# Two flamingo layers on one core: maxima of two score banks merged, w1's rounding constant on ScalarE, all orders rewritten

## The chip, the cores and the metric

One core of one Trainium2 chip. The metric is the device time of one execution of the kernel in microseconds, the median of several runs. Weights are raw inputs: their quantization and splitting are part of the time.

## The reference, cut to what matters

x is [2, 2048, 512] in float32. Two layers follow each other, each with a cross attention or mixing block and a feed-forward block, added with gates:

```python
x = x + tanh(g_xattn[0]) * attention(layernorm(x), ctx, Wq, Wkv, Wout)   # 8 heads, rotary, 128 context rows
x = x + tanh(g_ffn[0]) * ffn_relu2(layernorm(x), w_fc, w_proj, u, v, fast_b, gate)   # ternary weights, low rank part
x = x + tanh(g_xattn[1]) * (layernorm(x) @ W1.T + mean(ctx) @ W2.T + b)
x = x + tanh(g_ffn[1]) * bitlinear(gelu(bitlinear(layernorm(x), w1, b1)), w2, b2)
```

The score step is softmax(q k^T / 8) over the 128 context rows. In the last block bitlinear rounds its input, after an rms norm, to integers of -127 to 127 by the row's largest absolute value, and the weights to -1, 0 and 1.

## The kernel before, in words

The 4096 rows are worked in 16 groups of 256 rows, each of two tiles of 128 rows. For every group the steps are: layer norm 1, q projection, rotation, scores, softmax, values (pv), output projection (wo), layer norm 2, the low-rank part (low, low_sum), the up projection with relu squared in 8 chunks (up and up_rest), the down projection in 4 pieces per tile, layer norm 3, the mix projection (wx), layer norm 4 and rounding (x3_out, q4_out), w1 in 4 steps per tile, gelu and rounding, w2, and the store. Where float32 precision is wanted a tensor is kept as a high and a low part in float16, and three products are added. All the products write into 8 banks of PSUM.

Five engines work from five lists written out by hand: TensorE, VectorE (DVE), ScalarE (ACT), GpSimd (POOL), and the queue of SyncE (SP), which issues all loads, stores and DMA transposes. The table ORDER (from L334) gives for each engine, each step and each group the places of its tiles in that engine's list, and PREP the places of the preparation steps; each run() walks through the places and calls the step. Steps of three or four neighbouring groups are interleaved in this way, with the preparation of the weights (rounding to ternary, "lift" and "clip", the copy of lowA, the high part of wx) interleaved with groups 0 and 1. Every dependency is a semaphore wait in the step itself (need() and need_dma()), so that an engine that arrives early stands still, with its whole list behind it.

The steps that the change touches are these.

- Scores and softmax. `scores` (L1760) writes 4 units of scores into 4 banks, the four of each matmul round next to each other. `soft_max` (L1408, L1412) takes on VectorE for each unit the negated maximum of 4 heads and multiplies it by the scale; `exps` (L966) waits for the unit and takes 4 exponentials on ScalarE, and sums them. Then follow reciprocal, product on GpSimd (L781), float16 copy (L974), low part (L1382), and a DMA transpose ahead of pv.
- Ahead of the scores stands the rotation: three products on VectorE (L1395 to L1398), a sum on GpSimd (L771), the high part on ScalarE (L959), and the low part on VectorE (L1382).
- Rounding ahead of w1. `x3_out` (L1476 and on) adds the mix to the rows and takes statistics; `q4_out` scales the row (L1489 to L1496), multiplies it and adds 12582912 so that it is rounded (L1505), and subtracts the constant again into float16 (L1509). SP then transposes the result (`turn_q4`), and `w1_up` (L1904) uses it. `x3_hi` (L1023) is ScalarE's float16 copy of a tile of the same size. In the last group the transposes are done by TensorE (L1647), and the constant is subtracted by ScalarE behind them (L908).
- `ln3_apply` (L1378) writes the tile x3n that the rounding of the group before has read.

The other lines that come up: L1735 q projection, L1788 output projection, L1434 its sum on VectorE, L1801 and L1810 the low-rank matmuls with ScalarE's copies (L988, L992) and VectorE's rest (L1447), L1835 and L1841 up, L1002 relu on ScalarE, L1861 down, L776 low part of the hidden tile on GpSimd, L1883 mix, L1920 w2, L1556 the last sum of a tile.

Of the kernel before, what the change touches and what calls it, by code (L numbers as in the profile page):

```python
# [19 lines left out]
ACT = mybir.ActivationFunctionType  # L20
# [3 lines left out]
P = 128  # L24
# [24 lines left out]
def build(nc, x_d, ctxT_d, wqT_d, wkvT_d, woT_d, wfc_d, wproj_d, uT_d, wxT_d, wcT_d, bx_d, w1T_d, b1_d, w2T_d, b2_d,  # L49
          rope_d, small_d, out_d):  # L50
    ctx = ExitStack()
    with ctx:
# [173 lines left out]
        def mix_bank(g, n):  # L226
# [47 lines left out]
        turned_x3, turned_q4, turned_q5, end_x3lo, end_q4 = [sem(n) for n in (  # L274
            "turned_x3 turned_q4 turned_q5 end_x3lo end_q4").split()]
# [55 lines left out]
        def last_in(place):  # L331
# [18 lines left out]
                down=((45, 46, 48, 49, 47, 50, 51, 53), (77, 78, 81, 85, 80, 87, 89, 93),  # L350
# [13 lines left out]
                wo=((26, 27), (54, 55), (90, 91), (125, 126), (166, 167), (204, 205), (242, 243), (282, 283),
                    (320, 321), (361, 362), (399, 400), (438, 439), (476, 478), (517, 518), (558, 559), (594, 595)),
                low=((33,), (61,), (95,), (133,), (174,), (211,), (251,), (289,), (330,), (369,), (408,), (447,),
                     (486,), (524,), (564,), (603,)),
                wx=((58, 59), (94, 110), (136, 147), (172, 184), (216, 225), (250, 267), (292, 306), (333, 338),
                    (372, 379), (410, 418), (448, 457), (484, 497), (523, 537), (567, 575), (601, 606), (635, 636)),
                w1=((73, 74, 75, 76, 79, 82, 83, 86), (111, 112, 113, 115, 119, 120, 124, 130),  # L370
# [225 lines left out]
        def _(sp):  # L596
# [1408 lines left out]
```

## Time and profile before

| what | us |
|---|---|
| median of 3 runs | 1177.62 |
| lowest, highest | 1175.28, 1179.0 |
| the profiled execution, its own time | 1178.83 |
| its span in the profile | 1176.7 |
| TensorE busy in it | 1094.3 |
| VectorE busy | 953.5 |
| ScalarE busy | 799.4 |
| GpSimd busy | 591.5 |

The profile is of one execution. Busy times are shares of its span, 1176.7 us; the rest of the execution's own time, 2.1 us, lies around the span. A group of rows names a line of the kernel, the engine, what is written and read, the count, the busy time, the mean duration and the idle time just before, with the engine that ended it.

### The profile page before, as it was taken

The page shows a single profiled execution, that of the slowest core. Times are in us where ns is not written, and L with a number is a line of the kernel's source. Part 1 is how long each engine was busy: PE and PEld are TensorE (multiplying, and loading weights), DVE is VectorE, ACT ScalarE, POOL GpSimd, SP SyncE. Part 2 cuts the span into 40 slices and gives each one's busy share as a digit, 9 for nine tenths or more (in the row PEclk, how much of TensorE's full clock was granted, in tenths as well). Part 3 has the DMA queues.
Part 4 walks back from the last instruction along what each step waited for, and adds up shares of the span by engine and source line. Part 5 has one row for each costly group of instructions (what it writes and reads, how often), then busy time and mean ns, then how long its engine had stood idle before and what let it go on. Part 6 is the DMA issues. An engine that isn't in the chain of part 4 may idle for free.

```text
span 1176.7 us, 22172 instructions
## 1 busy us (share of the span) xinstructions
PE 1094.3 (93%) x8270; PEld 677.4 (58%) x8558; DVE 953.5 (81%) x1989; ACT 799.4 (68%) x1575; POOL 591.5 (50%) x567
## 2 busy tenths in 40 slices
PE   5776699999999999999899999999999999999997
PEld 5544456474655656475655656475656656564654
DVE  4796868778789888788878798898879886998667
ACT  3988947676683958576584857676674957586545
POOL 4243545464653746454544656555545555564431
PEclk9888799999999999999999999999999999999999
DMA  9959651434525343533625252443436242432210
GB/s 339 367 153 309 204 122 47 99 81 77 126 59 117 69 116 73 104 81 68 126 53 136 57 123 68 89 110 77 108 55 145 45 119 61 103 69 55 68 45 27
DMA packets 273802, 128.11 MB, mean 109 GB/s; under 512 B 247568, under 2 KB 248080, under 8 KB 272016
## 3 DMA queue, kind: packets, MB, share of 16 engines
q1 hardware_dynamic: 273136, 125.73, 41.8%
q8 instruction: 67, 1.10, 0.4%
q10 hardware_dynamic: 560, 0.96, 0.3%
q14 instruction: 39, 0.32, 0.1%
HBM read 57.19 MB, written 8.39 MB: 56 GB/s over the span
## 4 chain that ended last, share of the span: by engine, by line
PE 55%; ACT 17%; DVE 16%; POOL 5%; issue 4%; DMA 2%; SPq 0%; ACTq 0%; DVEq 0%
PE ps L1861 14%; PE ps L1835 10%; PE ps L1904 6%; PE ps L1920 5%; PE ps L1788 5%; ACT e L966 4%; PE ps L1735 4%; PE ps L1883 4%; ACT rl L1002 3%; ACT hid L1007 2%; ACT sq L1013 2%; PE ps L1760 1%; DVE st L1369 1%; PE ps L1841 1%; PE ps L1775 1%
## 5 line engine op out<-in xcount | busy, mean ns | idle before, releaser
L1835 PE MATMUL ps<-xT,fcT 128*128 128x256 f16 x2048 | 262.5, 276 | 10.8 <-ACT rl L1002 7.1
L749 POOL TENSOR_TENSOR rs<-ve,nhalf 128x1 f32<-128x1 f32 x160 | 101.7, 638 | 306.1 <-DVE ve L1374 222.8
L1861 PE MATMUL ps<-pjT,hid 128*128 128x512 fp8e4 x1024 | 232.3, 379 | 2.6 <-POOL hid L776 1.6
L1835 PEld LDWEIGHTS ps<-xT,fcT 128*128 128x128 fp8e4 x2048 | 200.1, 99 | 52.6 <-ACT rl L1002 10.0
L776 POOL TENSOR_TENSOR hid<-sq,hid 128x512 f16<-128x512 f32 x128 | 163.1, 1279 | 80.3 <-ACT sq L1013 79.4
L1861 PEld LDWEIGHTS ps<-pjT,hid 128*128 128x128 f16 x1024 | 98.0, 98 | 98.3
L1002 ACT ACTIVATE rl<-ps,rsf 128x256 f32<-128x256 f32 x256 | 106.4, 469 | 25.0 <-PE ps L1841 24.8
L966 ACT ACTIVATE e<-ps,nmb,sig 128x128 f32<-128x128 f32 x256 | 113.1, 462 | 7.2 <-DVE nmb L1412 6.9
L1904 PE MATMUL ps<-w1T,q4T 128*128 128x512 fp8e4 x480 | 114.2, 379 | 0.7 <-issue 0.6
L1058 ACT ACTIVATE q<-h 128x2048 f16<-128x2048 f32 x30 | 57.3, 1910 | 79.3 <-DVE h L1531 79.3
L781 POOL TENSOR_TENSOR e<-e,einv 128x512 f32<-128x512 f32 x64 | 70.1, 1100 | 78.5 <-DVE einv L1416 78.5
L1520 DVE SCALAR_TENSOR_TENSOR h<-ps,dqs,b1bc 128x512 f32<-128x512 f32 x120 | 87.4, 744 | 27.0 <-PE ps L1904 24.4
L1920 PE MATMUL ps<-w2T,hT 128*128 128x512 fp8e4 x480 | 108.5, 379 | 0.7 <-DMA hT<-q 0.7
L1735 PE MATMUL ps<-pt,wq 128*128 128x256 f16 x768 | 88.6, 275 | 4.4 <-DVE r L1434 3.0
L1788 PE MATMUL ps<-wo,qT 128*128 128x512 f16 x384 | 87.3, 384 | 4.4 <-DVE qT L1382 4.4
L1735 PEld LDWEIGHTS ps<-pt,wq 128*128 128x128 f16 x768 | 75.3, 99 | 18.4 <-issue 7.8
L1883 PE MATMUL ps<-wx,xT 128*128 128x512 f16 x360 | 82.5, 379 | 2.3 <-DVE r L1556 1.2
L1007 ACT ACTIVATE hid<-rl 128x512 f16<-128x512 f32 x128 | 80.6, 630 | 5.0
L1100 DVE TENSOR_REDUCE amax<-h 128x1 f32<-128x2048 f32 x30 | 68.4, 2280 | 13.4 <-ACT h L1027 13.3
L1013 ACT ACTIVATE sq<-rl 128x512 f32<-128x512 f32 x128 | 78.5, 613 | 0.0
L1920 PEld LDWEIGHTS ps<-w2T,hT 128*128 128x128 f16 x480 | 46.2, 98 | 50.7
L1382 DVE TENSOR_TENSOR p<-e,p 128x512 f16<-128x512 f32 x64 | 62.6, 993 | 14.0 <-ACT p L974 13.7
(243 smaller groups left out, 2025.7 us busy)
## 6 DMA issues: line engine op xcount, KB each, us to landing
xb<-in_x SPq DMA_DIRECT2D x16, 512.0 KB, 3.6
xa<-in_x SPq DMA_DIRECT2D x15, 512.0 KB, 4.0
out<-r SPq DMA_DIRECT2D x30, 256.0 KB, 2.3
rope<-in_rope SPq DMA_DIRECT2D x16, 384.0 KB, 3.2
h<-in_w1T SPq DMA_DIRECT2D x6, 1024.0 KB, 5.8
h<-in_w2T SPq DMA_DIRECT2D x6, 1024.0 KB, 6.4
h<-in_wkvT SPq DMA_DIRECT2D x2, 1024.0 KB, 12.6
hid<-in_w_fc SPq DMA_DIRECT2D x2, 1024.0 KB, 9.9
```

The costliest lines, as they stand in the source:

```text
L776: pool.tensor_tensor(flat[:, 1, :], sq[:, m % 2, :], flat[:, 0, :], ALU.subtract).then_inc(hid_lo, 1)
L966: last = act.activation(e[:, n, a * S:(a + 1) * S], s_bank(g, n)[:, a * S:(a + 1) * S], ACT.Exp, bias=nmb[:, n, a:a + 1], scale=sig[:, :], ...
L1002: act.activation(rl[:, m % 2, a * G:(a + 1) * G], ps[:, FFN0 + m % 2, a * G:(a + 1) * G], ACT.Relu, scale=rsf[:, 2 * m + a:2 * m + a + 1]) ...
L1007: act.activation(hid[:, 0, 2 * m:2 * m + 2, :].rearrange("p c n -> p (c n)"), rl[:, m % 2, :], ACT.Square)\
L1013: act.activation(sq[:, m % 2, :], rl[:, m % 2, :], ACT.Square).then_inc(sq_done, 1)
L1735: mm = pe.matmul(q_bank(hg)[:, a * G:(a + 1) * G], wq[:, ws, k, c:c + P], xT1[:, xs, k, :], start=(n == 0 and k == 0), stop=(n == 2 and k ...
L1788: mm = pe.matmul(wo_bank(t), ao[:, xs, k, t * P:(t + 1) * P], wo[:, ws, k, :], start=(n == 0 and k == 0), stop=(n == 2 and k == KC - 1))
L1835: pe.matmul(ps[:, FFN0 + m % 2, a * G:(a + 1) * G], fcT[:, k, f * P:(f + 1) * P], xT2[:, xs, k, :], start=(xs == 0 and k == 0), stop=False)
L1861: mm = pe.matmul(ps[:, FFN0 + t, :], hid[:, xs, c, t * P:(t + 1) * P], pjT[:, c, :], start=(c == 0 and xs == 0), stop=(c == FC - 1 and xs ...
L1883: mm = pe.matmul(mix_bank(g, t), xT3_of(g)[:, xs, k, t * P:(t + 1) * P], wx[:, ws, k, :], start=(n == 0 and k == 0), stop=(n == 2 and k == ...
L1904: mm = pe.matmul(mix_bank(g, 2 + u), q4T_of(g)[:, k, t * P:(t + 1) * P], w1T[:, k, n * 512:(n + 1) * 512], start=(k == 0), stop=(k == KC - 1))
L1920: mm = pe.matmul(mix_bank(g, 10 + t), hT_of(g)[:, t, c, :], w2T[:, c, :], start=(c == 0), stop=(c == FC - 1))
```

## The change

Three things are changed. The maxima of the third and fourth bank of scores (banks 2 and 3 of PSUM, which lie next to each other) are taken by one reduction of 128x1024 and one product, which raises the semaphore by two. The subtraction of the rounding constant ahead of w1 is taken from VectorE and done by ScalarE, as a copy with a bias, for all groups under one semaphore, q4_int; SP waits for it ahead of the transpose, and so does ln3_apply of the next group ahead of writing x3n. Every place in ORDER and PREP is written anew.

```diff
@@ -176,6 +176,9 @@
         return back_bank(g - 2, 0)
     return ps[:, ROW_TILES[j], :]
 
+def s_pair():
+    return slice(ROW_TILES[2], ROW_TILES[3] + 1)
+
 def pv_bank(a):
     return ps[:, (4, 2)[a], :]
 
@@ -271,8 +274,8 @@
 xT1_in, xT2_in, xT3_in, q4T_in, hT_in = [[sem(f"{n}{t}") for t in range(TILES)] for n in
                                          "xT1_in xT2_in xT3_in q4T_in hT_in".split()]
 p_in = [sem(f"p_in{n}") for n in range(4)]
-turned_x3, turned_q4, turned_q5, end_x3lo, end_q4 = [sem(n) for n in (
-    "turned_x3 turned_q4 turned_q5 end_x3lo end_q4").split()]
+turned_x3, turned_q4, turned_q5, end_x3lo, q4_int = [sem(n) for n in (
+    "turned_x3 turned_q4 turned_q5 end_x3lo q4_int").split()]
 END = GROUPS - 1
 TURN_Q5 = (0, 1, 5, 6)
 
@@ ORDER, TensorE @@
-s=((13,), (31,), (60,), (106,), (146,), (182,), (221,), (261,), (299,), (335,), (374,), (412,),
-   (451,), (494,), (536,), (571,)),
+s=((13,), (31,), (66,), (103,), (146,), (181,), (218,), (261,), (300,), (337,), (377,), (414,),
+   (456,), (493,), (537,), (571,)),
...
@@ ORDER, ScalarE @@
+q4=((90, 91), (128, 134), (158, 172), (196, 205), (229, 238), (264, 274), (296, 311), (332, 341),
+    (360, 368), (396, 406), (430, 443), (471, 475), (501, 513), (538, 546), (565, 573), (577, 579)),
...
@@ -662,7 +666,7 @@
         if final(g):
             return
         need(sp, w1_ps, 4 * TILES, g - 1, 4 * t + 3)
-        need(sp, q4_done, 2 * TILES, g, 2 * t + 1)
+        need(sp, q4_int, TILES, g, t)
         sp.dma_start_transpose(q4T[:, :, t * P:(t + 1) * P], q4[:, t, :]).then_inc(q4T_in[t], 16)
 
     def turn_q5(g, t):
@@ -903,10 +907,6 @@
                            accum_out=scf[:, done:done + 1]).then_inc(c_rows, 1)
 
     def prepare(p):
-        for t in here("ACT", "q4_end", p):
-            act.wait_ge(turned_q4, t + 1)
-            act.activation(q4T_of(END)[:, :, t * P:(t + 1) * P], chunks_of(FFN0 + t), ACT.Copy, bias=-MAGIC)\
-                .then_inc(end_q4, 1)
         for _ in here("ACT", "wq", p):
             weight_hi(0, 0, wq32, wq)
         for _ in here("ACT", "k_hi", p):
@@ -1022,6 +1022,15 @@
         need(act, xn3, TILES, g, t)
         act.activation(x16b[:, t, 0, :], x3n_of(g)[:, t, :], ACT.Copy).then_inc(x3hi, 1)
 
+    def q4_integers(g, t):
+        if final(g):
+            act.wait_ge(turned_q4, t + 1)
+            dst, src = q4T_of(g)[:, :, t * P:(t + 1) * P], chunks_of(FFN0 + t)
+        else:
+            need(act, q4_done, TILES, g, t)
+            dst, src = q4[:, t, :], x3n[:, t, :]
+        act.activation(dst, src, ACT.Copy, bias=-MAGIC).then_inc(q4_int, 1)
+
     def gelus(g, t):
         need(act, h_done, 4 * TILES, g, 4 * t + 3)
         act.activation(h_of(g)[:, t, :], h_of(g)[:, t, :], ACT.Gelu).then_inc(gelu, 1)
@@ -1079,6 +1088,8 @@
                 low_first(g)
             for t, g in due("ACT", "x3_hi", p):
                 x3_hi(g, t)
+            for t, g in due("ACT", "q4", p):
+                q4_integers(g, t)
             for t, g in due("ACT", "gelu", p):
                 if final(g):
                     gelu_quarters(g, t)
@@ -1403,13 +1414,18 @@
         lo(flat[:, 1, :], ropeu[:, hg, :], flat[:, 0, :], q_lo)
 
     def soft_max(g, n):
-        need(dve, s_ps, 4, g, n)
-        scores = s_bank(g, n).rearrange("p (h s) -> p h s", h=4)
-        dve.tensor_reduce(nmx[:, n, :], scores, axis=AX.X, op=ALU.max, negate=True).then_inc(s_max, 1)
+        units = slice(2, 4) if n == 2 else slice(n, n + 1)
+        need(dve, s_ps, 4, g, units.stop - 1)
+        if n == 2:
+            scores = ps[:, s_pair(), :].rearrange("p b (h s) -> p b h s", h=4)
+        else:
+            scores = s_bank(g, n).rearrange("p (h s) -> p h s", h=4).unsqueeze(1)
+        dve.tensor_reduce(nmx[:, units, :], scores, axis=AX.X, op=ALU.max, negate=True).then_inc(s_max, 1)
         if first(g) and n == 0:
             dve.wait_ge(c_kap, 1)
-        need(dve, s_max, 4, g, n)
-        dve.tensor_scalar(nmb[:, n, :], nmx[:, n, :], sig[:, :], None, ALU.mult).then_inc(s_bias, 1)
+        need(dve, s_max, 3, g, n)
+        dve.tensor_scalar(nmb[:, units, :], nmx[:, units, :], sig[:, :], None, ALU.mult)\
+            .then_inc(s_bias, units.stop - units.start)
 
     def soft_inv(g, n):
         need(dve, s_exp, 4, g, n)
@@ -1463,6 +1479,7 @@
         ln_stats(ln3, g, 2, t, r2_of(g)[:, t, :], 1.0, EPS)
 
     def ln3_apply(g, t):
+        need(dve, q4_int, TILES, g - 1, t)
         ln_apply(rs3, xn3, g, 2, t, r2_of(g)[:, t, :], x3n_of(g)[:, t, :])
 
 
@@ -1503,10 +1520,6 @@
         quant_scales(z4, 6 * t + 2, 6 * TILES, 0, g, t, rs4, 3, wmean[:, 0:1])
         z = x3n_of(g)[:, t, :]
         dve.tensor_scalar(z, z, qsc[:, 0, t:t + 1], MAGIC, ALU.mult, ALU.add).then_inc(q4_done, 1)
-        if final(g):
-            return
-        need(dve, q4_done, 2 * TILES, g, 2 * t)
-        dve.tensor_scalar(q4[:, t, :], z, MAGIC, None, ALU.subtract).then_inc(q4_done, 1)
 
     def h_out(g, t, n):
         need(dve, w1_ps, 4 * TILES, g, 4 * t + n)
@@ -1654,14 +1667,14 @@
             turn(FFN0 + t, x3n_of(END)[:, t, :], turned_x3)
         for t in here("PE", "q4_turn", p):
             pe.wait_ge(end_x3lo, t + 1)
-            need(pe, q4_done, 2 * TILES, END, t)
+            need(pe, q4_done, TILES, END, t)
             turn(FFN0 + t, x3n_of(END)[:, t, :], turned_q4)
         for u in here("PE", "q5_turn", p):
             t, n = u // 4, u % 4
             if t == 1:
                 need(pe, q5_done, TILES, END, n)
             elif n < 2:
-                pe.wait_ge(end_q4, n + 1)
+                need(pe, q4_int, TILES, END, n)
             else:
                 need(pe, out_done, TILES, END - 1, 1)
             need(pe, q5_round, TILES, END, u)
@@ -1896,7 +1909,7 @@
         elif not final(g) and not final(g + 1):
             need(pe, s_exp, 4, g + 2, 1)
         if n == 0 and final(g):
-            pe.wait_ge(end_q4, t + 1)
+            need(pe, q4_int, TILES, g, t)
         elif n == 0:
             need_dma(pe, q4T_in[t], g)
         pe.ldweights(q4T_of(g)[:, 0, t * P:(t + 1) * P], tile_position=(0, 0))
```

The tables, read as a sequence, give for TensorE between some steps (group behind the point; the steps stand in the order of the list):

```
between q1.8 and s.8:          before up1.7 up_rest1.7 up2.7             after up1.7 up_rest1.7 up2.7 up3.7
between low_sum and up1:       before nothing in 0, 13                   after nothing in 2, 12, 14
between wo1.2 and low.2:       before w2_0.0 down7.1 wx0.1               after down5.1 down6.1 w2_0.0 down7.1 wx0.1 q0.3 q1.3
between wx1.8 and w1_4.8:      before w1_0.8 w1_1.8 up3.9 up4.9 up5.9 up6.9 up7.9 w1_2.8 pv0.10 down0.9 w1_3.8
                               after  up2.9 up3.9 w1_0.8 w1_1.8 w1_2.8 w1_3.8 up4.9
from the last down step, before: x3_turn0 w2_0.14 x3_turn1 wx0.15 wx1.15 w2_1.14 q4_turn0 w1_0.15 w1_1.15 w1_2.15 q4_turn1
                               w1_3.15 w1_4.15 w1_5.15 w1_6.15 w1_7.15 q5_turn0..3 w2_0.15 q5_turn4..7 w2_1.15
from the last down step, after: wx0.15 w1_4.14 w1_5.14 w1_6.14 w1_7.14 x3_turn1 w2_0.14 wx1.15 q4_turn0 w1_0.15 w1_1.15 w1_2.15
                               w1_3.15 q4_turn1 w1_4.15 w1_5.15 w1_6.15 w1_7.15 w2_1.14 q5_turn0..3 w2_0.15 q5_turn4..7 w2_1.15
```

## Rows read from the trace of the kernel before

**Rows 1.** The page, busy time, share of the span and instructions of each engine

```profile
PE 1094.3 (93%) x8270; PEld 677.4 (58%) x8558; DVE 953.5 (81%) x1989; ACT 799.4 (68%) x1575; POOL 591.5 (50%) x567
```

**Rows 2.** Windows of three stages; columns: stretch, length, busy of PE, PEld, DVE, ACT, POOL, PEclk, DMA

```profile
0.00:150.00 150.00, 104.19 (x759) 73.63 (x761) 107.73 (x209) 119.00 (x228) 61.98 (x60) 0.86 0.83 273
150.00:1120.00 970.00, 941.92 (x7274) 577.82 (x7539) 807.04 (x1691) 654.65 (x1303) 517.52 (x494) 1.00 0.38 88
1120.00:1176.70 56.70, 48.14 (x242) 25.98 (x259) 38.74 (x91) 25.70 (x46) 12.03 (x14) 0.97 0.13 38
```

**Rows 3.** What TensorE waited for, 150 to 1120 us; columns: total, times, longest

```profile
PE ps L1760 <- DVE qT L1382: 5.9, 7, 2.0
PE ps L1835 <- ACT rl L1002: 2.9, 5, 1.4
PE ps L1788 <- DVE qT L1382: 2.6, 3, 1.1
...
PE ps L1861 <- POOL hid L776: 1.6, 3, 1.2
PE ps L1735 <- DVE r L1434: 1.5, 2, 0.9
...
PE ps L1883 <- DVE r L1556: 1.2, 2, 0.9
...
PE ps L1835 <- DVE tres L1447: 0.9, 1, 0.9
...
PE ps L1904 <- issue: 0.6, 1, 0.6
```

**Rows 4.** Groups by form; busy, mean ns, then idle before

```profile
L1408 DVE TENSOR_REDUCE nmx<-ps 128x4 f32<-128x512 f32 x64 | 43.6, 681 | 11.8 <-PE ps L1760 11.8
...
L1412 DVE TENSOR_SCALAR nmb<-nmx,sig 128x4 f32<-128x4 f32 x64 | 25.7, 401 | 2.4
...
L1509 DVE TENSOR_SCALAR x16b<-x3n 128x512 f16<-128x512 f32 x30 | 24.5, 817 | 1.0
...
L1023 ACT ACTIVATE x16b<-x3n 128x512 f16<-128x512 f32 x30 | 18.8, 626 | 53.6 <-DVE x3n L1378 53.6
...
L1100 DVE TENSOR_REDUCE kvmax<-ps 128x1 f32<-128x1024 f32 x1 | 1.2, 1225 | 0.5 <-PE ps L1684 0.5
```

**Rows 5.** Line 1509 alone: ns at least, median, at most

```profile
L1509 DVE TENSOR_SCALAR x16b<-x3n x30: 426/428/1376, 187.7 to 1103.8; 128x512 f16<-128x512 f32 x30
```

**Rows 6.** Timeline of group 8 ahead of its scores; columns: start, length, instructions

```profile
580.69 1.46 POOL L771 TENSOR_TENSOR e<-e 128x512 f32<-128x512 f32 x1
581.05 1.38 DVE L1509 TENSOR_SCALAR x16b<-x3n 128x512 f16<-128x512 f32 x1
...
583.78 2.48 PE L1760 MATMUL ps<-k,qT 32*128 32x128 f16 x96 [2.03 <-DVE qT L1382]
```

**Rows 7.** The chain of waits, one unit's exps on ScalarE

```profile
458.91 1.76 ACT e L966 x8
```

**Rows 8.** The chain by time, 210 to 240 us; columns: start, length, what

```profile
218.38 1.73 PE ps L1861 x8
...
235.90 2.05 issue
```

**Rows 9.** TensorE's timeline in group 13, behind the low-rank sum

```profile
963.27 1.05 PE L1835 MATMUL ps<-xT,fcT 128*128 128x256 f16 x8 [0.94 <-DVE tres L1447]
```

**Rows 10.** What TensorE waited for, 0 to 150 us

```profile
PE ps L1835 <- ACT rl L1002: 4.2, 2, 2.7
```

**Rows 11.** The window from 120 to 150 us, columns as rows 2

```profile
120.00:150.00 30.00, 22.28 (x153) 16.46 (x155) 23.82 (x23) 29.76 (x61) 17.59 (x11) 0.77 0.75 208
```

**Rows 12.** Timeline of TensorE in the tail

```profile
1144.43 3.62 PE L1920 MATMUL ps<-w2T,hT 128*128 128x512 fp8e4 x16
...
1151.82 0.60 PE L1647 MATMUL ps<-ident,e 128*128 128x128 f32 x4
...
1161.31 3.44 PE L1647 MATMUL ps<-ident,hid 128*128 128x128 f32 x16 [4.47 <-DVE hid L1550]
```

More of the change, by code:

```diff
@@ L364, in build @@
[L364 to L369, printed above, removed]
@@ new lines, in build @@
+                low_sum=((33,), (61,), (99,), (135,), (175,), (215,), (252,), (291,), (332,), (371,), (411,),
+                         (450,), (489,), (525,), (567,), (603,)),
+                up_rest=((36, 37), (64, 65), (101, 102), (138, 139), (178, 180), (219, 220), (256, 258), (293, 297),
+                         (335, 336), (375, 376), (413, 416), (452, 454), (491, 492), (528, 529), (569, 570),
+                         (606, 607)),
+                up=((34, 35, 38, 39, 40, 42, 43, 44), (62, 63, 67, 68, 76, 78, 79, 80),
[7 rows of a table added]
@@ new lines, in build @@
+                wo=((24, 26), (54, 55), (88, 89), (127, 128), (165, 166), (204, 205), (242, 243), (281, 282),
+                    (320, 321), (361, 362), (400, 401), (439, 440), (478, 479), (516, 517), (558, 560), (595, 596)),
+                low=((32,), (60,), (97,), (133,), (173,), (214,), (250,), (289,), (330,), (369,), (409,), (448,),
+                     (487,), (523,), (565,), (601,)),
+                wx=((56, 59), (94, 107), (136, 148), (176, 185), (216, 224), (257, 266), (292, 306), (331, 341),
+                    (367, 378), (406, 418), (444, 458), (484, 497), (526, 539), (564, 576), (604, 615), (629, 636)),
@@ L545, in build @@
                        (329, 330))))
         PREP = dict(
-            PE=dict(x3_turn=(632, 634), q4_turn=(638, 642), q5_turn=(648, 649, 650, 651, 653, 654, 655, 656),
-                    k=(2, 3), v=(5, 6), low=(0,), mix=(14,), tern=(4, 10, 11, 15, 19, 20, 21, 22), low_t=(16,),
-                    row_scale=(24,), mean=(30,), spread=(1, 8, 12, 18, 25)),
-            DVE=dict(x3lo_end=(814, 817), ctx_sum=(7,), rot_k=(10, 11), wq_max=(3,), wq_scale=(6,), k_max=(13,),
-                     wq_lo=(8,), v_max=(19,), kv_scale=(23,), k_lo=(29,), v_lo=(34, 35), low_copy=(5,),
-                     thr=(9, 15, 20, 37, 46, 48, 49, 52), wo_max=(12,), v_top=(22,), wo_scale=(26,), wo_lo=(30,),
-                     mix_row=(43,), low_rank=(42,), v_parts=(28,), wx_max=(53,), hidden=(54,), wx_scale=(58,),
-                     wx_lo=(88,), row_scale=(56,), mean=(71,), diag=(55,), round=(72, 78, 81, 89, 90, 95, 97, 101),
-                     clip=(79, 85, 86, 91, 94, 98, 100, 103)),
@@ L556, in build @@
-            ACT=dict(q4_end=(548, 549), wq=(3,), k_hi=(17,), v_hi=(19, 20), tanh=(1,), wo=(18,),
-                     evac=(6, 14, 15, 29, 33, 35, 36, 37), rows=(4, 7, 10, 21), whole=(5, 8, 12, 28), low=(32,),
-                     wx=(46,), sums=(39, 40, 41, 42, 43, 44, 45, 47), lift=(54, 61, 62, 67, 71, 76, 79, 80)),
-            POOL=dict(whole=(18, 19, 20, 21), rot_k=(5, 6), csb=(4,), low_zero=(13,)),
-            SP=dict(u=(0,), rows=(16,), ctx=(2,), wk=(3,), wq=(1,), wv=(7,),
-                    piece=(4, 5, 10, 18, 19, 15, 22, 24, 27, 29, 31, 32, 33, 36, 37, 38, 40, 41, 45, 47, 48, 50, 52, 55),
-                    wo=(6,), wc=(14,), wx=(13,), b1=(17,)))
+            PE=dict(x3_turn=(627, 634), q4_turn=(637, 642), q5_turn=(648, 649, 650, 651, 653, 654, 655, 656),
+                    k=(2, 3), v=(5, 6), low=(0,), mix=(14,), tern=(4, 9, 10, 15, 17, 18, 19, 21), low_t=(22,),
+                    row_scale=(30,), mean=(29,), spread=(1, 11, 12, 23, 25)),
@@ new lines, in build @@
+            DVE=dict(x3lo_end=(790, 799), ctx_sum=(13,), rot_k=(9, 10), wq_max=(3,), wq_scale=(6,), k_max=(12,),
+                     wq_lo=(7,), v_max=(18,), kv_scale=(24,), k_lo=(28,), v_lo=(26, 36), low_copy=(5,),
+                     thr=(8, 14, 20, 35, 43, 44, 47, 48), wo_max=(11,), v_top=(23,), wo_scale=(25,), wo_lo=(31,),
+                     mix_row=(49,), low_rank=(51,), v_parts=(30,), wx_max=(53,), hidden=(54,), wx_scale=(69,),
+                     wx_lo=(80,), row_scale=(75,), mean=(64,), diag=(55,), round=(67, 72, 78, 86, 90, 91, 94, 102),
+                     clip=(73, 83, 87, 88, 92, 97, 99, 104)),
@@ new lines, in build @@
+            ACT=dict(wq=(3,), k_hi=(18,), v_hi=(17, 19), tanh=(1,), wo=(20,), evac=(6, 13, 14, 31, 32, 33, 35, 36),
+                     rows=(4, 7, 9, 21), whole=(5, 8, 11, 28), low=(48,), wx=(53,),
+                     sums=(38, 39, 40, 41, 42, 43, 45, 46), lift=(52, 61, 66, 67, 72, 78, 79, 82)),
+            POOL=dict(whole=(18, 19, 20, 21), rot_k=(4, 5), csb=(6,), low_zero=(13,)),
+            SP=dict(u=(0,), rows=(13,), ctx=(2,), wk=(3,), wq=(1,), wv=(5,),
+                    piece=(4, 7, 11, 20, 19, 16, 22, 24, 28, 30, 31, 32, 35, 36, 37, 38, 39, 42, 45, 47, 49, 50, 52, 55),
+                    wo=(6,), wc=(18,), wx=(14,), b1=(17,)))
```

258 lines of the change are left out of this document (127 added, 131 removed), and 123 rows, old and new, of tables (down, exp, h, hid).

## The prediction

> **What bounds the kernel now.** I read the busy shares first, then a table by stage, then what TensorE waited for. TensorE is busy 93% of the span, VectorE 81%, ScalarE 68% [rows 1]. The stages say more [rows 2]: the first 150 us, in which weights are loaded and quantized, leave TensorE idle for 150.0 - 104.2 = 45.8 us; the 970 us from 150 to 1120 leave it idle for only 28.1 us; the last 56.7 us for 8.6 us. The granted clock is 1.00 in the long middle, which is the 2.4 GHz level, and 0.86 in the first stage. All orders are rewritten but TensorE does the same matmuls, so a new order can win only from idle time and from the clock of the first stage. In the middle the pot is 28 us, spread over many waits of 0.2 to 2 us [rows 3]: 5.9 for the low part of q ahead of the scores, 2.6 for the low part ahead of the output projection, 2.9 for ScalarE's relu, 0.9 in the low-rank chain, and so on down to single DMA or issue waits. So this is a TensorE-bound kernel with thin stalls, and a VectorE that is cheaper by some per cent saves nothing by itself.
>
> **Part 1, rounding constant to ScalarE.** VectorE loses 30 subtractions at 817 ns, 24.5 us; ScalarE gains 30 copies with a bias. The nearest row is the copy of the same tile and shape at 626 ns, 18.8 us [rows 4]. Over the middle ScalarE works 654.7 of 970 us, so 18.8 us more fit; VectorE falls from 807 towards 783 us. What is late on the path is another matter. The chain is x3_out, statistics, q4_out, integers, transpose, w1. It now has one more hand-over, but 0.63 us in place of 0.82. The mean of 817 ns hides two cases: the median is 428 ns, the longest 1376 ns [rows 5]. In group 8's timeline the instruction starts at 581.05 inside a GpSimd addition (580.69 to 582.15), takes 1.38 us and ends 0.28 us after it; the low part of q stands behind it on VectorE, and TensorE then sits 2.03 us ahead of the scores [rows 6]. 30 x (817 - 428) = 11.7 us of VectorE's 24.5 are such waits. The page SBUF — State Buffer of the Trainium skill, section "SBUF: two separate sides", says that VectorE and GpSimd share one port pair under an exclusive lock, so that either blocks the other for a whole instruction. By that rule GpSimd gets time back too, and the gain would be the third rival's and not mine; the trace agrees as far as VectorE's side goes, 1.38 against 0.43 us.
>
> New waits: the transpose of q4 on SP waits for ScalarE instead of VectorE, and behind it in SP's queue stand the next transposes. ln3_apply of the next group now waits for ScalarE's integers of this one, with all of VectorE's list behind it; those integers precede this group's w1, whose results VectorE needs long before that, so I cost it at 0. Without that cover it is 0.63 us per tile. The last group's integers were on ScalarE before: 0.
>
> **Part 2, one maximum for banks 3 and 4.** 16 times, two reductions of 681 ns and two products of 401 ns become one of each. The reduction of 128x1024 from PSUM stands in the trace once, at 1225 ns [rows 4], so it saves 16 x (2 x 681 - 1225) = 2.2 us; the products save 16 x 401 = 6.4 us. The four banks of scores are finished by neighbouring matmuls, so no wait is added. The third exp starts 1225 - 681 = 0.54 us later and the fourth earlier; the unit before keeps ScalarE busy for 1.76 us [rows 7] and covers that. If ScalarE sat idle there it would cost 16 x 0.54 = 8.7 us at worst; VectorE's saving lies beside TensorE: 0 on the path. Both parts take 24.5 + 8.6 = 33.1 us (3.5%) from VectorE.
>
> **Part 3, the orders.** This decides. No row shows the new order, so I measured each dependency by its cover: the TensorE steps listed between producer and user, at the chain's rates (8 down matmuls of 512 columns 1.73 us [rows 8], so 0.216 each and 0.108 for 256 columns; an up chunk has 18 of these, 1.95). Against cover stands the latency seen in the old order.
> - q to scores: cover on the mean of groups 1 to 14 from 5.2 to 6.5 us, the smallest from 1.5 to 3.0. Group 8, 2.03 us late, gets one more up chunk (1.95). I take -3.0 of the 5.9; ends -5.9 and 0.
> - Values to output projection: smallest cover 0.9 to 1.7, mean 3.0 to 3.3: -1.3 of 2.6; ends -2.6 and +1.
> - Low-rank chain: the second up chunk stands right behind low_sum in one group before (13, a wait of 0.94 us [rows 9]) and in three now (2, 12, 14): +2.0; ends 0 and +3.
> - Output projection to low: smallest cover 7.7 before (group 2, 2.05 us of issue in the chain [rows 8]), 8.5 now (3 and 15): 0; ends -2 and +3.
> - Other places where VectorE is the releaser (1.5 + 1.2 + 0.9 [rows 3]), with 3.5% less before it: -1.5; ends -3.6 and 0.
> - Start: TensorE waits 4.2 us there for the relus of group 0 [rows 10], ScalarE being busy 29.76 of the 30 us from 120 [rows 11]. The new list of ScalarE has one 2.0 us lift and one p_hi fewer ahead of the last relu, but moves the copy of lowA and wx's high part towards that place: -2.0; ends -6 and +4.
> - Tail: the second w2 of group 14 now stands between the last w1 and the turns of q5, where TensorE waits 4.47 us [rows 12], and lasts 3.45: up to -3.5. But four w1 steps of group 14 come after the last down steps of group 15, and between the last mix and the second q4 turn there are now one turn and four w1 steps, 0.45 + 4 x 0.86 = 3.9 us; in the old order this stretch ran from 1144.43 to 1151.82, 7.4 us, with a w2 in it. I take +1.0; ends -3.5 and +5.
> Sum: -3.0 - 1.3 + 2.0 - 1.5 - 2.0 + 1.0 = -4.8, say -5. It is made against the profiled execution, 1178.83 us (span 1176.7), which stands 1.2 us above the median of the runs: 1177.6 - 5 = 1172.6 us.
>
> **Rivals.** About 0.3% (3.5 us) is what a measurement of this kernel can tell from no change: 1174.1 to 1181.2 is "same".
> - *New stalls in place of old ones*: the old order's 28 us in the middle are single waits at changing places; a rewritten order has its own. For it: VectorE is the releaser of 5.9 + 2.6 + 1.5 + 1.2 + 0.9 = 12.1 us of the 28.1; three zero covers stand where one was. Against: the covers of the two largest VectorE waits grew. Time: 1177.6.
> - *Slower: the w1 matmuls wait for ScalarE.* The integers now stand in ScalarE's list behind a unit's exps (1.76 us [rows 7]) or a gelu. In the old order covers down to 10.5 us between wx and w1 of tile 1 left no wait but 0.6 us of issue [rows 3]; in the new one the smallest are 9.2 (group 8), 10.2 (2), 10.5 (1 and 5), 11.1 (3 and 11). If each integer step comes 2.0 us late, they lack 3.3 + 2.3 + 2 x 2.0 + 2 x 1.4 = 12.4 us: 1172.6 + 12.4 = 1185. From 1.4 us of lateness (8.8 us) it outweighs my gain by enough to be read as slower. Against: ScalarE is idle 315 of the middle's 970 us [rows 2], and the copy is 0.19 us shorter than the subtraction that it replaces [rows 4].
> - *Larger gain*: if VectorE's instructions have slowed GpSimd's as GpSimd's slow VectorE's, both become faster, and all waits of the middle on q, wo, r, tres and hid vanish: 5.9 + 2.6 + 1.5 + 1.2 + 0.9 + 1.6 = 13.7; with start and tail as above, 14.7: 1163. For it: an instruction of 428 ns that takes up to 1376. Against: hid's waits have been 1.6 us only. The lock in the page named above would work this way.
> - That the change doesn't do what it says: the exps read the merged result by unit as before, so I see no room for it, and give it nothing.
>
> **Numbers.** Forecast (1167 to 1174) 0.40, larger gain 0.12, same 0.32, slower 0.16. So faster 0.52. The range 1163 to 1183 leaves out half of the large gain and most of the slower case, about 0.15. The likeliest case's own range is 1167 to 1174.
>
> **What would show it.** VectorE busy near 920 us and ScalarE near 818; the fp16 subtraction gone, a 626 ns copy in its place; 16 reductions near 1.2 us. Idle of TensorE in the middle near 24 us, waits ahead of the scores near 3 us. The tail: no 4.5 us wait at the turns of q5, a new one of some 3 us at q4's. I am wrong if w1 waits for q4T, if the zero covers cost over 1 us each, or if the first stage moves by more than 5 us.

## The result, and the profile after

The changed kernel takes 1183.37 us (median of 6 runs, 1182.73 to 1184.83) beside 1176.24 for the one before in the same session: ratio 1.0062, 95% interval 1.0045 to 1.0079. It is slower by some 7 us. The prediction was 1172.6, faster. The profiled execution took 1184.36 us, with a span of 1182.2.

The page of the changed kernel, its busy shares:

```profile
span 1182.2 us, 22186 instructions
PE 1092.8 (92%) x8270; PEld 670.5 (57%) x8558; DVE 927.5 (78%) x1927; ACT 814.7 (69%) x1605; POOL 577.7 (49%) x567
```

The parts did most of what was foreseen. VectorE lost 26.0 us against [rows 1], not the 33.1 forecast; ScalarE gained 15.3; TensorE did the same work. The next view groups the instructions by form (line, output <- input, count, busy time, mean ns, idle before), first ScalarE, then VectorE:

```profile
L1032 ACT ACTIVATE x16b<-x3n 128x512 f16<-128x512 f32 x30 | 18.7, 624 | 9.0 <-DVE x3n L1522 9.0
...
L1423 DVE TENSOR_REDUCE nmx<-ps 128x4 f32<-128x512 f32 x32 | 21.9, 684 | 14.3 <-PE ps L1773 14.2
L1423 DVE TENSOR_REDUCE nmx<-ps 128x8 f32<-128x1024 f32 x16 | 19.4, 1213 | 0.0
L1427 DVE TENSOR_SCALAR nmb<-nmx,sig 128x4 f32<-128x4 f32 x32 | 17.3, 542 | 1.2
L1427 DVE TENSOR_SCALAR nmb<-nmx,sig 128x8 f32<-128x8 f32 x16 | 5.5, 345 | 1.7
```

The integers take ScalarE 624 ns a tile where 626 was taken for them, and the merged maximum 1213 where 1225 was taken. The small products saved 2.9 us and not 6.4 (17.3 + 5.5 against 25.7 [rows 4]): one for a single bank takes 542 ns on the mean here, 401 before. The stages, in the columns of [rows 2]:

```profile
0.00:150.00 150.00, 101.25 (x756) 72.41 (x756) 103.52 (x200) 113.92 (x216) 53.60 (x58) 0.89 0.82 261
150.00:1120.00 970.00, 939.70 (x7259) 572.32 (x7522) 776.54 (x1619) 670.96 (x1341) 512.29 (x496) 1.00 0.38 89
1120.00:1182.20 62.20, 51.79 (x258) 25.80 (x281) 47.47 (x109) 29.81 (x49) 11.84 (x14) 1.00 0.13 36
```

TensorE is idle for 48.8 us in the first stage (45.8 before), 30.3 in the middle (28.1; forecast 24) and 10.4 behind it (8.6). The first stage was hardly slower for it (by 0.6 us, in the table below): its granted clock is 0.89 in place of 0.86. What TensorE waited for between 150 and 1120 us (us in total, times, longest), against [rows 3]:

```profile
PE ps L1773 <- DVE qT L1393: 5.1, 3, 4.0
PE ps L1814 <- issue: 3.8, 5, 1.2
PE ps L1848 <- DVE tres L1463: 3.1, 4, 1.0
PE ps L1896 <- DMA xT<-x16b: 2.3, 2, 1.3
PE ps L1874 <- issue: 2.3, 1, 2.3
PE ps L1848 <- ACT rl L1002: 2.3, 3, 1.4
PE ps L1896 <- DVE r L1569: 2.1, 4, 0.9
PE ps L1917 <- DVE h L1533: 2.0, 3, 1.1
PE ps L1748 <- DVE r L1450: 1.8, 1, 1.8
...
PE ps L1801 <- DVE qT L1393: 1.1, 2, 0.6
```

The many short waits ahead of the scores (7) became 3, but one of them is 4.0 us long. Of the four waits in the low-rank chain, three stand at the zero covers of groups 2, 12 and 14 (0.93, 0.94 and 1.03 us in TensorE's timeline), the fourth is 0.22. No row above blames ScalarE for more than it did before, and the whole view has no wait for q4T: from it alone nobody would find the cause.

To see where the time goes I use **lost time**: at a mark, the time minus what the matmuls done until then would take at the chain's full rate (0.216 us for 512 columns; float32 ones weighted fourfold). All kernels here do the same matmuls, so only differences between kernels are read from it. Worked out from the matmul groups up to each mark:

| mark, us | 150 | 200 | 650 | 1100 | end of span |
|---|---|---|---|---|---|
| before | 38.4 | 42.5 | 76.7 | 98.5 | 105.3 |
| changed kernel | 39.0 | 49.4 | 73.8 | 102.3 | 110.8 |

The changed kernel loses 6.3 us between 150 and 200, gains 9.8 until 650, and loses 6.7 between 650 and 1100.

### The profile page after: what moved, and what is told of

It reads as the page before. It is cut to its first block, busy times and chain, and to the rows that moved or that the text cites. A ratio compares the mean times of both kernels' runs of the same rounds, so it can differ in the third digit from the quotient of the medians.

```text
span 1182.2 us, 22186 instructions
## 1 busy us (share of the span) xinstructions
PE 1092.8 (92%) x8270; PEld 670.5 (57%) x8558; DVE 927.5 (78%) x1927; ACT 814.7 (69%) x1605; POOL 577.7 (49%) x567
## 4 chain that ended last, share of the span: by engine, by line
PE 56%; DVE 17%; ACT 16%; issue 5%; DMA 4%; POOL 1%; SPq 0%; ACTq 0%; POOLq 0%; DVEq 0%
PE ps L1874 14%; PE ps L1848 11%; PE ps L1917 6%; PE ps L1801 5%; PE ps L1933 5%; PE ps L1748 4%; ACT e L966 4%; PE ps L1896 4%; ACT rl L1002 2%; ACT hid L1007 2%; DVE st L1380 2%; ACT sq L1013 1%; PE ps L1854 1%; PE ps L1788 1%; DMA h<-in_w2T 1%
## 5 line engine op out<-in xcount | busy, mean ns | idle before, releaser
L1848 PE MATMUL ps<-xT,fcT 128*128 128x256 f16 x2048 | 261.0, 275 | 7.9 <-ACT rl L1002 4.5
L1848 PEld LDWEIGHTS ps<-xT,fcT 128*128 128x128 fp8e4 x2048 | 197.6, 98 | 51.9 <-ACT rl L1002 8.3
L780 POOL TENSOR_TENSOR hid<-sq,hid 128x512 f16<-128x512 f32 x128 | 155.4, 1217 | 102.3 <-ACT sq L1013 101.9
L1393 DVE TENSOR_TENSOR p<-e,p 128x512 f16<-128x512 f32 x64 | 64.8, 1022 | 26.0 <-ACT p L974 25.7
```

What stands on the lines that cost most here:

```text
L780: pool.tensor_tensor(flat[:, 1, :], sq[:, m % 2, :], flat[:, 0, :], ALU.subtract).then_inc(hid_lo, 1)
L1848: pe.matmul(ps[:, FFN0 + m % 2, a * G:(a + 1) * G], fcT[:, k, f * P:(f + 1) * P], xT2[:, xs, k, :], start=(xs == 0 and k == 0), stop=False)
```

## The experiments

Each is timed beside the kernel before, whose median was 1176.0 to 1177.9 in the five sessions, so the ratios are what is compared. A run's label stands where it is introduced. "Old orders" are those of the kernel before, "new orders" those of the changed one; "the constant" is w1's rounding constant.

**Orders and parts taken apart.** First the new orders with neither part (e_orders): VectorE subtracts, four maxima.

```diff
-q4_integers(g, t) on ScalarE for every group
+dve.tensor_scalar(q4[:, t, :], z, MAGIC, None, ALU.subtract).then_inc(q4_int, 1)   # behind q4_out's rounding
-one reduction of s_pair()
+soft_max(g, 2); soft_max(g, 3)
```

> The new orders of every engine, with neither of the other two parts: the maxima are taken bank by bank again (the third and fourth at the same place), and VectorE takes the rounding constant off again. Theory 'the orders lose it': with VectorE 33 us busier the new orders do no better than in the changed kernel, 1184 to 1189 us. Theory 'ScalarE's extra step in the chain loses it': without it the new orders are at or under the time of before, 1172 to 1178 us.

Measured: 1189.97 us, ratio 1.0108 [1.0091, 1.0126]. Then the reverse (e_parts), both parts in the old orders, each of ScalarE's copies put into its list where the subtraction had ended in the trace of before:

```diff
 ORDER = the old places
-dve.tensor_scalar(q4[:, t, :], z, MAGIC, None, ALU.subtract)
+act.activation(q4[:, t, :], x3n[:, t, :], ACT.Copy, bias=-MAGIC).then_inc(q4_int, 1)
+the merged soft_max(g, 2)
```

> The old orders with both parts: one maximum for the third and fourth bank at the place of the third, and ScalarE taking the constant off at the place in its old list that came next once VectorE's rounding had ended in the trace of before. Theory 'the orders lose it': the parts alone are harmless or help, 1170 to 1176 us. Theory 'ScalarE's extra step loses it': 1180 to 1186 us, with waits ahead of w1 or of the scores.

Measured: 1186.38, ratio 1.0086 [1.0069, 1.0102]. So the parts cost in the old orders, and the new orders cost without the parts; together they cost far less than the sum of the two.

**The two parts one by one**, in the old orders. The merged maximum alone (e_max):

```diff
 ORDER = the old places
-soft_max(g, 2); soft_max(g, 3)
+the merged soft_max(g, 2)
```

> The old orders with the merged maximum alone. The old orders with both parts took 1186.4 us, 9.5 over before. Theory 'ScalarE's list': this part adds nothing to ScalarE, so 1173 to 1179 us. Rival 'the later third exp': the third exp starts 0.5 us later in 16 groups, so 1180 to 1186 us.

Measured: 1176.28, ratio 0.9987 [0.9973, 1.0000]. Nothing that can be told from none, as costed. The constant on ScalarE alone (e_int):

```diff
 ORDER = the old places
-dve.tensor_scalar(q4[:, t, :], z, MAGIC, None, ALU.subtract)
+act.activation(q4[:, t, :], x3n[:, t, :], ACT.Copy, bias=-MAGIC).then_inc(q4_int, 1)
```

> The old orders with the rounding constant taken off by ScalarE alone. Theory 'ScalarE's list': the copy of 0.63 us, and the wait for VectorE ahead of it, stand in front of relus that TensorE needs at the pace of one chunk in 1.95 us while ScalarE takes 2.18 us for one, so this part carries nearly all of the 9.5 us: 1183 to 1187 us. Rival 'both parts share it': 1180 to 1182 us. Rival 'the merged maximum': 1175 to 1179 us.

Measured: 1185.64, ratio 1.0067 [1.0049, 1.0084]. This is the part that costs. TensorE's waits in the middle of this run (its L1763 is up, L1789 down, L1832 w1):

```profile
PE ps L1763 <- ACT rl L920: 4.8, 8, 1.3
PE ps L1811 <- DMA xT<-x16b: 2.8, 2, 1.7
PE ps L1789 <- POOL hid L698: 2.6, 3, 1.2
...
PE ps L1789 <- ACT rl L920: 1.9, 5, 0.8
...
PE ps L1832 <- DMA q4T<-x16b: 1.7, 1, 1.7
```

The relus were 2.9 ahead of up and hid 1.6 [rows 3]; for the relus ahead of down the kernel before has

```profile
PE ps L1861 <- ACT rl L1002: 1.0, 2, 0.7
```

There are two readings: the copies make ScalarE's other work late, or the hand-over makes q4 late (the 1.7 us for q4T was not there before).

**Busy time or hand-over?** VectorE keeps its subtraction; ScalarE gets a copy of a dead tile at the same 30 places, bound to nothing of the group (e_dummy):

```diff
+act.activation(bxbc[:, :], bxbc[:, :], ACT.Copy, bias=-1.0)   # where e_int has q4_integers
```

> The old orders, and neither part of the change: VectorE takes the constant off, with its own subtraction, and the maxima stay four. Added is only work for ScalarE: at the 30 places of its list at which the kernel with the constant on ScalarE has its copies, it copies a dead fp32 tile of 128x512 onto itself with a bias, waiting for nothing of this group. The output stays the reference's. Theory 1, ScalarE's 18.4 us of extra busy time push its later work (relus, qT, lowsum) back: 1183 to 1187 us, as in the kernel with the constant on ScalarE alone (1185.6). Theory 2, the hand-over costs (q4's integers come later, so its transposes and w1 do): 1175 to 1179, as before. My own guess is between, nearer to theory 1: 1182, because TensorE's waits for the relus grew from 7.1 to 9.9 us there.

Measured: 1185.88, ratio 1.0073 [1.0055, 1.0092]: the whole loss of e_int, with no hand-over in it. Its ScalarE, the real float16 copy and the dummy:

```profile
L941 ACT ACTIVATE x16b<-x3n 128x512 f16<-128x512 f32 x30 | 18.8, 627 | 54.2 <-DVE x3n L1309 54.2
L950 ACT ACTIVATE bxbc<-bxbc 128x512 f32<-128x512 f32 x30 | 18.6, 619 | 0.0
```

The waits of TensorE in its middle (L1769 is up, L1795 down, L1838 w1), and below them its window from 150 to 1120 (the columns of [rows 2]):

```profile
PE ps L1769 <- ACT rl L920: 4.6, 8, 1.9
PE ps L1795 <- POOL hid L698: 3.0, 4, 1.2
...
PE ps L1795 <- ACT rl L920: 2.1, 5, 0.8
...
PE ps L1838 <- DMA q4T<-x16b: 1.4, 2, 0.8
```

```profile
150.00:1120.00 970.00, 935.37 (x7232) 570.29 (x7495) 796.20 (x1682) 664.07 (x1323) 517.53 (x493) 1.00 0.38 88
```

Idle grew from 28.1 to 34.6 us, 6.5. The relus' waits went from 2.9 + 1.0 to 4.6 + 2.1, hid's (which is made of ScalarE's square) from 1.6 to 3.0: 4.2 of the 6.5. The wait for q4T is there too, 1.4 us, with no hand-over behind it; so its coming up in e_int is no sign of one. The chain that ended last says it most clearly. Its shares by engine, in the kernel before, with the dummies, and with the constant on ScalarE alone:

```profile
PE 55%; ACT 17%; DVE 16%; POOL 5%; issue 4%; DMA 2%; SPq 0%; ACTq 0%; DVEq 0%
```

```profile
PE 41%; ACT 26%; DVE 18%; POOL 6%; issue 5%; DMA 2%; SPq 0%; ACTq 0%; DVEq 0%
```

```profile
PE 44%; ACT 23%; DVE 20%; POOL 5%; issue 5%; DMA 2%; SPq 1%; ACTq 0%; DVEq 0%
```

ScalarE holds a quarter of the chain as soon as the 18.6 us are in its list; in e_max, where they are not, it holds 18%. A likely reason can be read from its forms in the kernel before, which no row ahead of the prediction showed:

```profile
L1002 ACT ACTIVATE rl<-ps,rsf 128x256 f32<-128x256 f32 x256 | 106.4, 469 | 25.0 <-PE ps L1841 24.8
L1007 ACT ACTIVATE hid<-rl 128x512 f16<-128x512 f32 x128 | 80.6, 630 | 5.0
L1013 ACT ACTIVATE sq<-rl 128x512 f32<-128x512 f32 x128 | 78.5, 613 | 0.0
```

An up chunk costs ScalarE 2 x 0.469 + 0.630 + 0.613 = 2.18 us, and TensorE 1.95. ScalarE is the slower of the two in each of the 128 chunks, however idle it is over the whole. The growth of the waits for its relus and squares fits this. That the chunks are where the copies hurt was not tested by itself.

**What the exchange could have won.** The other side: nobody takes the constant off. The rounding of w1's integers is left out in groups 0 to 14; VectorE writes the scaled value straight into the float16 tile (e_free). This takes away the second instruction and its hand-over together.

```diff
-dve.tensor_scalar(z, z, qsc[:, 0, t:t + 1], MAGIC, ALU.mult, ALU.add).then_inc(q4_done, 1)
+dve.tensor_scalar(q4[:, t, :], z, qsc[:, 0, t:t + 1], 0.0, ALU.mult, ALU.add).then_inc(q4_done, 1)
```

> Left out: the rounding of w1's integers in groups 0 to 14, so that the output is not the reference's. VectorE writes the scaled value straight to the fp16 tile, with no constant added and none taken off; nobody does a second instruction. Old orders, merged maximum. So VectorE is 33 us lighter than in the kernel before and ScalarE unchanged: what the change could have won at most in these orders. The merged maximum alone took 1176.3. If VectorE's time is worth nothing by itself: 1175 to 1177. If its releases carry a part of the middle's idle time: 1171 to 1174. I expect 1174.5, because the chain to w1 is shorter too.

Measured: 1175.06, ratio 0.9991 [0.9979, 1.0003]. In the new orders (e_freenew):

```diff
-ORDER = the old places
+ORDER = the new places
```

> The same omission in the new orders, which the changed kernel has: it is the changed kernel without ScalarE's 28 to 30 copies. With them it took 1183.4, with the constant on VectorE 1185.5. If ScalarE's copies cost here as they do in the old orders: 1183.4 - 8 = 1175. If the new orders have made room for them: 1181 to 1183. I expect 1180, since the new orders lose their time in the first 200 us and the tail whoever takes the constant off.

Measured: 1176.38, ratio 1.0002 [0.9991, 1.0014]. And the new orders with the merged maximum, the constant on VectorE (e_newmax):

```diff
 ORDER = the new places, the merged soft_max(g, 2)
-q4_integers(g, t) on ScalarE
+dve.tensor_scalar(q4[:, t, :], z, MAGIC, None, ALU.subtract).then_inc(q4_int, 1)
```

> The new orders with the merged maximum, and the constant on VectorE as before. The new orders with neither part took 1190.0, with both 1183.4. Theory 1, the new orders owe their 6.6 us to the constant having left VectorE, whose place in the new list of VectorE is too tight for it: 1188 to 1190. Theory 2, it is the merged maximum, or ScalarE's share of the copies costs as much here as in the old orders (some 9 us) and the maximum gives it back: 1176 to 1182. I expect theory 1: 1189.

Measured: 1185.53, ratio 1.0077 [1.0055, 1.0099]; in neither theory's range. All six kernels below have the merged maximum:

| constant taken off by | nobody | VectorE | ScalarE |
|---|---|---|---|
| old orders | 0.9991 | 0.9987 | 1.0086 |
| new orders | 1.0002 | 1.0077 | 1.0062 |

In the old orders the subtraction on VectorE costs nothing that can be measured, and on ScalarE 11 us. In the new ones it costs 7 us on ScalarE and 9 on VectorE, two figures that the intervals don't tell apart. So the new orders have no room for this instruction on either engine. VectorE's new list was written without it, which may be why it costs there; no run tests that. The middle of e_freenew, that is the changed kernel without ScalarE's copies:

```profile
150.00:1120.00 970.00, 945.62 (x7300) 578.28 (x7567) 774.47 (x1629) 657.42 (x1310) 515.51 (x497) 1.00 0.38 89
```

Idle 24.4 us, the 24 of the forecast. In the changed kernel it is 30.3: ScalarE's 18.7 us take 5.9 of it back, in this stage alone, spread over waits of all kinds: TensorE's waits for relus at up are 1.3 us in e_freenew and 2.3 in the changed kernel, those for the sums at q 0.4 and 1.8, those for the mix's transposes 1.2 and 2.3. The chain of e_freenew has 8% of ScalarE, that of the changed kernel 16%:

```profile
PE 60%; DVE 20%; ACT 8%; issue 5%; DMA 4%; POOL 3%; SPq 0%; ACTq 0%; POOLq 0%; DVEq 0%
```

```profile
PE 56%; DVE 17%; ACT 16%; issue 5%; DMA 4%; POOL 1%; SPq 0%; ACTq 0%; POOLq 0%; DVEq 0%
```

**Where ScalarE's time hurts.** Three kernels in the old orders. The 14 copies of groups 0 to 6 on ScalarE, the rest on VectorE (four maxima; e_early):

```diff
+SOME = tiles of groups 0 to 6    # q4_integers on ScalarE for these, VectorE for the rest
```

> The old orders, the four maxima as before, and the constant on ScalarE for the tiles of groups 0 to 6 alone (14 copies, at the places that they have with all on ScalarE); groups 7 to 14 stay on VectorE. If ScalarE's extra time is paid for wherever it stands (8.4 us over 30 copies, 0.28 each): 14 x 0.28 = 3.9 us, 1180.5. If it is paid for only in the second half, as the lost time counted from TensorE's work says (by 650 us the kernel with all 30 had lost nothing): 1176 to 1177.5. I expect the second: 1176.5.

Measured: 1181.42, ratio 1.0048 [1.0033, 1.0063]. My theory that only the second half pays fell. The 16 copies of groups 7 to 14 (e_late):

```diff
+SOME = tiles of groups 7 to 14
```

> The mirror of it: old orders, four maxima, the constant on ScalarE for groups 7 to 14 of it alone (16 copies of groups 7 to 14), groups 0 to 6 on VectorE. Paid for alike everywhere: 16 x 0.28 = 4.5 us, 1181. Paid for in the second half only: 1184 to 1186. I expect 1184.5.

Measured: 1184.01, ratio 1.0068 [1.0053, 1.0084]. Per copy that is 0.40 and 0.50 us. The two halves together are more than e_int's 30 copies cost (1.0067), so the cost isn't a sum over copies; why it saturates stays open. Last, six copies alone, each placed where ScalarE sat idle in the trace of before (merged maximum; e_some):

```diff
+SOME = ((2, 0), (3, 0), (6, 0), (9, 0), (12, 0), (14, 0))   # the other 24 tiles stay on VectorE
```

> The old orders with the merged maximum, and the constant moved to ScalarE for only six tiles (tile 0 of groups 2, 3, 6, 9, 12 and 14), each at a place where ScalarE stood idle in the trace of before; the other 24 stay on VectorE. If what costs is ScalarE's busy time at full places, these six cost nothing and take 6 x 0.8 = 4.9 us off VectorE: 1173 to 1176.5. If each hand-over costs by itself (9 us over 30 tiles, 0.3 each): 1178. I expect 1175, no clear gain over before.

Measured: 1178.01, ratio 1.0003 [0.9988, 1.0019]. At 0.28 to 0.5 us each they would have cost 1.7 to 3.0 us above the 0.9987 of e_max; measured are 1.9, with intervals as wide as that. So whether a copy in a gap is free isn't settled; that it wins nothing is.

**The orders in pieces**, with both parts. Old up to 200 us of before's trace, new behind it (h_oldstart):

```diff
+every engine's list: steps begun before 200 us in before's trace, old order; then the rest, new order
```

> Both parts; every engine first takes the steps that had begun by 200 us in the trace of before, in the old order, then all others in the new order. The new kernel stands 6.9 us further behind its own matmul work at 200 us than the old one, but part of this is made good by 240 us (3.7 us). Theory 'the start loses 3 to 7 us': 1177 to 1180 us. Theory 'the loss is in the later groups (from 700 us on) and the tail': no change from the changed kernel, 1182 to 1185 us.

Measured: 1181.44, ratio 1.0043 [1.0027, 1.0059]; between the two theories. New start, old orders behind (h_newstart):

```diff
+every engine's list: steps begun before 200 us in the changed kernel's trace, new order; then the rest, old order
```

> Both parts; the mirror of the run before: the steps that had begun by 200 us in the trace after the change in the new order, all others in the old order. Theory 'the start loses it': 1177 to 1182 us, 3 to 7 us over the run with the old orders and both parts. Theory 'the later groups lose it': within 1.5 us of that run.

Measured: 1191.88, ratio 1.0128 [1.0113, 1.0143]. With new orders behind, the new start costs 2 us (1.0062 against 1.0043, with intervals that overlap); with old orders behind, 5 us (1.0128 against 1.0086). One piece of it is a single place. In the changed kernel TensorE spreads the key scales only behind the two ternary steps (VectorE's timeline: start, duration, what, [idle before]):

```profile
50.24 0.48 DVE L1135 TENSOR_SCALAR r<-ident,wmax 128x128 f32<-128x128 f32 x2 [4.93 <-PE ps L1654]
```

Put back between the halves of group 0's q (e_spread):

```diff
 TensorE's list
-... q(0, 0), q(0, 1), tern_1, tern_2, spread_1
+... q(0, 0), spread_1, q(0, 1), tern_1, tern_2
```

> The changed kernel with one TensorE step put back: the product that spreads the maxima of k and v (spread 1) stands between the two halves of group 0's q projection again, instead of behind two ternary steps. Theory 'this step is what makes the start late': VectorE's wait of 4.9 us ahead of it goes and the whole gets 2 to 4 us faster, 1179 to 1181.5 us. Rival 'the start is held by something else (sums, transposes)': 1182.5 to 1184.5 us.

Measured: 1182.19, ratio 1.0040 [1.0025, 1.0054], 2.2 of a thousand below the changed kernel, with intervals that overlap, and between the two theories. The trace is clearer: VectorE's wait of 4.9 us is gone, and group 2's scores start 2.7 us earlier. The other piece of the start is the wait ahead of these scores. It is the same in both, first in the changed kernel, then in e_spread; in the kernel before it was 0.2 us:

```profile
192.74 1.79 PE L1773 MATMUL ps<-k,qT 32*128 32x128 f16 x96 [3.99 <-DVE qT L1393]
```

```profile
190.05 1.97 PE L1691 MATMUL ps<-k,qT 32*128 32x128 f16 x96 [3.99 <-DVE qT L1311]
```

Then the old start, the new orders to 650 us, and the old ones behind (h_mid):

```diff
+old order to 200 us, new order to 650 us, then the rest in the old order
```

> Both parts; old order for the steps begun by 200 us, new order for those begun by 650 us in the trace after the change, old order for the rest. Behind its own matmul work the new order lost 22.5 us from 200 to 600 us, the old one with both parts 32.6, and from 600 to 1165 us the new one 36.0, the old one with both parts 33.0. Theory 'the stretches add up': 41.7 + 22.5 to 27 + 33 and the end as in the old orders give 9 to 13 us under 1186.4, so 1174 to 1178 us. Rival 'joints and neighbours decide, not stretches': 1180 us or more.

Measured: 1180.56, ratio 1.0031 [1.0017, 1.0046], so the stretches don't add up: the rival's side. And the same with the constant on ScalarE for groups 0 to 6 only (h_best), my candidate to beat both kernels:

```diff
 the lists of the kernel above
+SOME = tiles of groups 0 to 6    # the rest on VectorE
```

> A candidate to beat both: the old orders up to 200 us, the new ones from there to 650, the old ones again behind that; merged maximum throughout; the constant on ScalarE for groups 0 to 6 and on VectorE behind them. The same orders with the constant on ScalarE throughout took 1180.6. By the lost time counted at marks: 2.9 us less than before at 650 us, and as before from there: 1176.5 - 2.9 = 1173.6. If the constant's place is not what costs in the last part, it stays at 1180. I expect 1174.

Measured: 1176.56, ratio 1.0006 [0.9990, 1.0023]. Taking the late copies off ScalarE gives 3 us back (0.0025, the intervals just overlapping). The result ties with before and doesn't beat it. No version here does.

## Why the prediction was wrong

- **The step that failed** is Part 1's "18.8 us more fit", drawn from ScalarE's busy share of the middle, with the integers costed at 0 by a cover for q4 alone. I asked whether w1 would get q4 in time, and never what stood behind the copy in ScalarE's list. The copies cost 7.0 us in the new orders (1183.4 against 1176.4) and 11 in the old ones (0.0095), at the forecast size of 0.62 us each. With this term the forecast would have been 1172.6 + 7 = 1179.6, no gain.
- **The second step that failed** is Part 3's -5 for the orders, at which the forecast stood 0.0042 under before. Measured is 0.0062 above, a miss of 0.0104, of which the copies are 0.0060. The other 0.0044, some 5 us, is this term: with nobody taking the constant off, the new orders are at 1.0002 beside 0.9991 for the old ones. They gained nothing that can be measured, and with the constant on VectorE they lost (1.0077).
- **The slower rival** gave the time nearly right (1185) with the wrong place. It had w1 waiting for late integers. With the same 30 copies bound to nothing, the loss was the same, and in the changed kernel's middle TensorE has no wait for q4T at all. Nor does VectorE wait there for ScalarE's integers ahead of ln3_apply, the wait that was costed at 0. The dummy kernel decides in the old orders; in the new ones it wasn't tried, and there e_freenew takes load and hand-over away together. Of the prediction's three signs of being wrong none came clearly: no wait for q4T, zero covers of 0.93 to 1.03 us, 0.6 us in the first stage. All three looked elsewhere than at ScalarE's list.
- **VectorE's 33 us** were worth little to nothing: 0.9991 with nobody doing the work. This much was said ("saves nothing by itself"), and -1.5 was taken for it all the same. The merged maximum at 0 was right.
- **Middle**: -3.8 for q, values, low-rank chain and VectorE's other waits together; without ScalarE's load it is 24.4 - 28.1 = -3.7, of which 1.1 is there in the old orders too (e_free's middle has 27.0). These are single executions, and e_freenew's was the fastest of its 12, 2.3 us under their median. The single terms were less exact: the scores' waits fell by 0.8 and not 3.0, wo's by 1.5 (-1.3), tres rose by 2.2 (+2.0). Of zero covers the old order had two, in groups 0 and 13, where the prediction counts one (group 0's lies in the first stage). The sum is right partly by luck.
- **Start**: -2.0 forecast. Lost time is +0.6 at 150 us, so the stage itself gained nothing, and +6.9 at 200, where the low part of group 2's rotated q comes late (the wait of 3.99 us). I had measured covers as means over groups 1 to 14 and gave group 2 nothing of its own.
- **Tail**: +1.0 forecast, 10.4 - 8.6 = +1.8. The 4.5 us wait is gone, as said; in its place are small ones, the largest three of them 1.4 to 1.5:

```profile
PE ps L1917 <- ACT qT L1032: 1.5, 2, 0.8
PE ps L1660 <- DVE e L1389: 1.4, 1, 1.4
PE ps L1917 <- DVE hid L1533: 1.4, 1, 1.4
```

- **The larger gain** fell. GpSimd's additions didn't get faster when VectorE's subtraction left: in e_int its busy time is 590.5 us against 591.5 [rows 1]. The page:

```profile
PE 1092.3 (92%) x8270; PEld 673.0 (57%) x8558; DVE 928.0 (78%) x1959; ACT 815.0 (69%) x1605; POOL 590.5 (50%) x567
```

  Its 577.7 in the changed kernel come with the new orders (579.7 with nobody subtracting). Some of GpSimd's additions do take longer than others of the same form, up to 2158 ns in the kernel before; but taking these 30 subtractions away moved the whole by 1.0 us:

```profile
L753 POOL TENSOR_TENSOR x16f<-rl,x16f x32: 1143/1162/2158, 110.5 to 1085.7; 128x512 f16<-128x512 f32 x32
```

  The Trainium skill, page SBUF — State Buffer, section "SBUF: two separate sides", has ScalarE on ports that wait for nobody. The trace agrees: 26 of the 30 copies overlap a GpSimd instruction, and all take 612 to 654 ns, where VectorE's subtraction took 426 to 1376 [rows 5]:

```profile
L1032 ACT ACTIVATE x16b<-x3n x30: 612/614/654, 187.7 to 1134.5; 128x512 f16<-128x512 f32 x30
```

## What to carry to other kernels

Before work is moved to an engine "with room", ask for its rate inside the inner loop that it shares with the bounding engine: ScalarE was 68% busy over the whole, but took 2.18 us against TensorE's 1.95 in every up chunk, and there the waits grew when it got more to do. A dummy of the same length at the same places tells in one run whether the load or the hand-over costs, and leaving the work out tells what the move could ever have won (here nothing); both are cheaper than writing new orders. An order written for one set of durations should be judged with each variant of the work (nobody, old engine, new engine) in both orders, for the two interact: 1.0108 and 1.0086 alone, 1.0062 together.

## What I had not expected

- 18.6 us of copies that depend on nothing cost 0.0073 of the time, some 8 us, of a kernel whose ScalarE is idle for a third of the time.
- The cause hardly shows in the waits of the changed kernel: TensorE's waits for ScalarE's relus in the middle are shorter there (2.3 us at L1848) than before (2.9 [rows 3]), and yet 7 us go when the copies do. Only beside e_freenew (1.3 us) do they show. The waits are booked to whoever came last by a little; the kernels without the copies tell what made that one late.
- 14 copies cost 0.0048, 16 others 0.0068, all 30 of them 0.0067.
